# Cross-attention and quantised feed-forward on one core: x normalised in rows and passed through a scratch in device memory

## What is computed

```python
def _layernorm(x, axis=-1, eps=1e-05):
    ...
x = x + _L0_xattn_ref(_layernorm(x), ctx, ctx, w, b, mask)
#   scores = einsum('bqd,bkd->bqk', q1, key) / 0.72
#   attn = softmax(scores) * drop_mask
#   (einsum('bqk,bkd->bqd', attn, value) + bias) @ weights
x = x + _L0_ffn_ref(_layernorm(x), weight_q, weight_scale, ffn_bias)
#   x rounded row by row to 8-bit integers, times weight_q.T, scaled back
```

## Time and profile before

| | us |
|---|---|
| three runs, median (lowest to highest) | 340.8 (340.61 to 341.39) |
| the profiled execution | 341.07 |
| its span from first to last instruction | 339.3 |
| PE busy | 329.1 (97%) |
| DVE busy | 308.6 (91%) |
| ACT busy | 226.8 (67%) |
| POOL busy | 236.4 (70%) |
| DMA queue of SP, share of 16 engines | 51.9% |

### The profile page before, as it was taken

The page is one execution under the profiler, slowest core; times in us unless marked ns, Lnnn a source line. Parts: engine busy times, 40 slices in busy tenths (PEclk is TensorE's granted clock), DMA queues, the critical chain, the costliest instruction groups (busy, mean ns, idle before and its releaser), DMA issues.

```text
span 339.3 us, 6055 instructions
## 1 busy us (share of the span) xinstructions
PE 329.1 (97%) x1574; PEld 263.3 (78%) x1574; DVE 308.6 (91%) x630; ACT 226.8 (67%) x455; POOL 236.4 (70%) x368
## 2 busy tenths in 40 slices
PE   6999999999999999999999999999999999999992
PEld 6988777778777788877778887777888877787781
DVE  3697899999899999999999999999999999999887
ACT  4456676766667786666777767667776666777651
POOL 4175567778777777877777787877777877767642
PEclk9999999999999999999999999999999999999999
DMA  7939854445665544556654555565454556400002
GB/s 237 285 100 251 183 139 117 121 127 163 128 172 153 139 148 123 160 133 170 169 139 131 135 153 140 153 170 150 130 136 140 151 143 170 139 33 31 31 33 94
DMA packets 64545, 47.67 MB, mean 140 GB/s; under 512 B 20112, under 2 KB 51088, under 8 KB 64528
## 3 DMA queue, kind: packets, MB, share of 16 engines
q1 hardware_dynamic: 64528, 47.47, 51.9%
HBM read 35.13 MB, written 8.39 MB: 128 GB/s over the span
## 4 chain that ended last, share of the span: by engine, by line
PE 70%; DVE 9%; issue 1%; ACT 1%; DMA 1%; DVEq 0%; SPq 0%
PE ps_attn L515 7%; PE ps_scores L515 7%; PE ps_scores L517 7%; PE ps_scores L516 7%; PE ps_attn L517 7%; PE ps_attn L516 7%; PE ps_ffn L676 7%; PE ps_vw L515 6%; PE ps_vw L516 6%; PE ps_vw L517 6%; PE ps_pt L507 3%; DVE ffn_out L950 1%; DVE abs_max L963 1%; DMA xq_t<-x_int 1%; PE ps_xt L599 1%
## 5 line engine op out<-in xcount | busy, mean ns | idle before, releaser
L752 ACT ACTIVATE x_norm<-x_blocks,norm_spread 128x128 f32<-128x128 f32 x124 | 51.2, 483 | 2.3 <-ACT norm_spread L745 1.5
L1206 POOL TENSOR_TENSOR ct_lo<-ct_raw,ct_hi 128x512 fp32r<-128x512 f32 x28 | 36.3, 1298 | 23.0 <-ACT ct_hi L730 23.0
L515 PE MATMUL ps_attn<-vw_hi,pt_hi 128*128 128x512 f32 x124 | 51.4, 415 | 0.0
L515 PE MATMUL ps_vw<-w_hi,ct_hi 128*128 128x512 f32 x116 | 50.7, 437 | 0.0
L1159 POOL TENSOR_TENSOR scaled<-meanvar,scale 128x2 f32<-128x2 f32 x32 | 16.6, 517 | 46.6 <-DVE meanvar L913 46.6
L515 PE MATMUL ps_scores<-ct_hi,xt_hi 128*128 128x512 f32 x124 | 48.7, 393 | 0.0
L517 PE MATMUL ps_scores<-ct_hi,xt_lo 128*128 128x512 f32 x124 | 48.5, 391 | 0.0
L516 PE MATMUL ps_scores<-ct_lo,xt_hi 128*128 128x512 f32 x124 | 48.4, 391 | 0.0
L517 PE MATMUL ps_attn<-vw_hi,pt_lo 128*128 128x512 f32 x124 | 48.4, 390 | 0.0
L516 PE MATMUL ps_attn<-vw_lo,pt_hi 128*128 128x512 f32 x124 | 48.3, 389 | 0.0
L854 ACT ACTIVATE x_neg<-x,meanvar 128x512 f32<-128x512 f32 x31 | 22.5, 724 | 38.6 <-DVE meanvar L1122 38.6
(11 more groups left out here) (164 smaller groups left out, 779.5 us busy)
## 6 DMA issues: line engine op xcount, KB each, us to landing
x_in<-in_x_dram SPq DMA_DIRECT2D x32, 256.0 KB, 3.1
mask_in<-in_mask_BxSxS_fk_dram SPq DMA_DIRECT2D x32, 256.0 KB, 3.7
out_dram<-out_tile SPq DMA_DIRECT2D x31, 256.0 KB, 2.2
x_blocks<-in_x_dram SPq DMA_DIRECT2D x60, 128.0 KB, 3.6
ctx_in<-in_ctx_dram SPq DMA_DIRECT2D x56, 128.0 KB, 2.8
ctx_in<-in_ctx_dram SPq DMA_DIRECT2D x4, 256.0 KB, 4.6
x_blocks<-in_L_xattn_weights_dram SPq DMA_DIRECT2D x4, 256.0 KB, 6.5
xq_t<-x_int SPq DMA_TRANSPOSE x26, 2.4
```

Source lines behind the costliest of these rows:

```text
L515: nc.tensor.matmul(bank_, lhs_hi(t), rhs_hi(t), start=(t == 0), stop=False)
L752: last = nc.scalar.activation(x_norm[:, k, a * P:(a + 1) * P], x_blocks[:, slot(n, 4), a * P:(a + 1) * P], ACT.Identity, bias=norm1_spread ...
L1206: nc.gpsimd.tensor_tensor(ct_lo[:, batch_of(n), :, j * P:(j + 1) * P], ct_raw[:, slot(n, 2), :, :], ct_hi[:, batch_of(n), :, j * P:(j + 1) ...
```

## The change

x is no longer loaded a second time. ACT normalises `x_in` in rows, in one instruction of 512 columns with the row's own mean and scale, three tiles ahead of the step, behind `pt_hi` where it stood ahead of it. SP stores the 64K numbers of the tile into `norm_rows`, a scratch in device memory (`store_rows`), behind the mask of the same step; at the beginning of its next step, behind the DMA of the integers, it waits for that store and loads the tile back with its blocks exchanged (`load_rows`, four DMAs of 64 KB for each tile where there were four of 128 KB for two). DVE turns `x_blocks` directly. The matmul L599, ACT's copy L745, POOL's `norm1_masked` (L1175) and the two constants behind them are gone. POOL gets two waits for `x_norm_ready`, of tiles n - 4 and d. (The `skipped` argument goes because only the context still uses `wait_pair`; its numbers stay.)

```diff
-def wait_pair(eng, sems, base, n, skipped=0):
-    uses = (PHASE + n) // 4 + 1 - skipped
+def wait_pair(eng, sems, base, n):
+    uses = (PHASE + n) // 4
     eng.wait_ge(sems[slot(n, 4) // 2], base * (4 * QUADS) + (16 * uses - 4 * PHASE) * QUADS)
+def wait_blocks(eng, sems, base, n):
+    eng.wait_ge(sems[slot(n, 2)], base * (8 * QUADS) + 8 * QUADS * (n + n % 2))
+def wait_rows(eng, sem, base, n):
+    if isinstance(base, int):
+        if base + n > 0:
+            eng.wait_ge(sem, 16 * (base + n))
+    else:
+        assert LOOP_FIRST + n > 0
+        eng.wait_ge(sem, base * 16 + 16 * n)
...
+    norm_rows = nc.dram_tensor("norm_rows", [TILES * P, D], F32, kind="Internal").ap()
...
+            def store_rows(base, n, row):
+                wait_count(sp, x_norm_ready, base, n + 1)
+                sp.dma_start(norm_rows[bass.ds(row, P), :], x_norm[:, slot(n, 2), :]).then_inc(norm_rows_stored, 16)
+            def load_rows(base, n, row):
+                quads = norm_rows[bass.ds(row, P), :].rearrange("(a i) d -> i a d", i=BLOCK)
+                wait_rows(sp, norm_rows_stored, base, n)
+                for b in range(QUADS):
+                    blocks = x_blocks[b * BLOCK:(b + 1) * BLOCK, slot(n, 4), :]
+                    sp.dma_start(blocks.rearrange("i (a c) -> i a c", a=QUADS),
+                                 quads[:, :, b * P:(b + 1) * P]).then_inc(x_blocks_loaded[slot(n, 2)], 16)
...
+            store_rows(0, 1, 1 * P)
             sp.wait_ge(w_lo_ready, NT)
             sp.wait_ge(bias_terms_ready, NT)
-            load_blocks(x_blocks, x_rows, 1 * P, 1, 1, x_blocks_loaded)
-            load_blocks(x_blocks, x_rows, 2 * P, 2, 2, x_blocks_loaded)
+            load_rows(0, 1, 1 * P)
...
+                n = d + 1
+                if exists(base, n) and not is_tile(base, n, 1):
+                    load_rows(base, n, row + n * P)
...
-                n = d + 3
-                if n % 2 == 0 and exists(base, n):
-                    wait_count(sp, x_norm_ready, base, n - 4 + 2)
-                    load_blocks(x_blocks, x_rows, row + n * P, n, 2, x_blocks_loaded)
...
+                n = d + 2
+                if exists(base, n):
+                    store_rows(base, n, row + n * P)
...
-                def spread_norm(n):
-                    wait_count(pe, norm1_masked_ready, base, n)
-                    wait_count(pe, norm1_spread_ready, base, n - 1)
-                    nc.tensor.matmul(ps_xt[:, 0:2 * QUADS], same_lane[:, :],
-                                     norm1_masked[:, slot(n, 2), :, :].rearrange("p a c -> p (a c)"),
-                                     start=True, stop=True).then_inc(spread_done, 1)
-                if is_tile(base, d, 0):
-                    pe.wait_ge(xt_lo_ready, 1)
-                    pe.wait_ge(same_lane_ready, 2 * QUADS - 1)
-                    spread_norm(d + 1)
-                elif exists(base, d + 2):
-                    spread_norm(d + 2)
...
-            def normalise_first():
-                act.wait_ge(norm1_ready, 1)
-                nc.scalar.activation(x_norm[:, 0, :], x_in[:, 0, :], ACT.Identity, bias=norm1[:, 0, 1:2],
-                                     scale=norm1[:, 0, 0:1]).then_inc(x_norm_ready, 1)
             def normalise(base, n):
-                k = slot(n, 2)
-                wait_count(act, spread_done, base, n)
-                wait_count(act, x_norm_ready, base, n - 1)
-                nc.scalar.activation(norm1_spread[:, k, :, :].rearrange("p a c -> p (a c)"), ps_xt[:, 0:2 * QUADS],
-                                     ACT.Copy).then_inc(norm1_spread_ready, 1)
-                wait_count(act, norm1_spread_ready, base, n)
-                wait_pair(act, x_blocks_loaded, base, n)
-                wait_count(act, xt_raw_ready, base, n - 2)
-                for a in range(QUADS):
-                    last = nc.scalar.activation(x_norm[:, k, a * P:(a + 1) * P],
-                                                x_blocks[:, slot(n, 4), a * P:(a + 1) * P], ACT.Identity,
-                                                bias=norm1_spread[:, k, a, 1:2],
-                                                scale=norm1_spread[:, k, a, 0:1])
-                last.then_inc(x_norm_ready, 1)
+                k = slot(n, 4)
+                wait_count(act, norm1_ready, base, n + 1)
+                wait_rows(act, norm_rows_stored, base, n - 2)
+                nc.scalar.activation(x_norm[:, slot(n, 2), :], x_in[:, slot(n, 8), :], ACT.Identity,
+                                     bias=norm1[:, k, 1:2], scale=norm1[:, k, 0:1]).then_inc(x_norm_ready, 1)
...
+            normalise(HEAD, PER_BATCH + 1)
...
-                    normalise(base, d + 1)
+                    normalise(base, d + 2)
...
-                if exists(base, d + 2):
-                    normalise(base, d + 2)
...
+                if exists(base, d + 3):
+                    normalise(base, d + 3)
...
-                wait_count(dve, x_norm_ready, base, n + 1)
+                wait_blocks(dve, x_blocks_loaded, base, n)
                 wait_count(dve, xt_lo_ready, base, n - 1)
-                turn_blocks(xt_raw[:, slot(n, 2), :, :], x_norm[:, slot(n, 2), :], xt_raw_ready)
+                turn_blocks(xt_raw[:, slot(n, 2), :, :], x_blocks[:, slot(n, 4), :], xt_raw_ready)
...
+                wait_count(pool, x_norm_ready, base, n - 4 + 1)
...
-                wait_count(pool, spread_done, base, n - 2)
-                nc.gpsimd.tensor_tensor(norm1_masked[:, slot(n, 2), :, :],
-                                        norm1[:, k, :].rearrange("p (a c) -> p a c", a=1).to_broadcast([P, QUADS, 2]),
-                                        own_block[:, :, :], ALU.mult).then_inc(norm1_masked_ready, 1)
...
-                        pool.wait_ge(x_norm_ready, 1)
+                    wait_count(pool, x_norm_ready, base, d + 1)
...
```

31 lines of the change are left out of this document (4 added, 27 removed).

## The result

| | before | after |
|---|---|---|
| median of its runs | 340.83 (340.61 to 341.39, 4 runs) | 345.61 (343.48 to 347.46, 4 runs) |
| the profiled execution | 341.07 | 343.48 |
| span | 339.3 | 341.7 |

The ratio of the times is 1.014, with a 95% interval of 1.008 to 1.020: the changed kernel is slower, by 4.8 us at the median. The prediction had the sign, with 342.1 and a range to 345.5; the median lies 0.1 us beyond the range and 3.5 above the forecast. The profiled execution, against which the sum was made, is the fastest of the four: 1.4 us above the sum's 342.07. It accounts for the first part of the miss; the second, 2.1 us between it and the median, has no trace of its own. Two single runs in the experiments, 348.4 us of e7_head_store_first and 345.2 of the kernel before beside e4_store_first, fell in the chip's slower state, and the ratios leave them out.

What follows compares the result with a forecast made beforehand. PE was taken to bound the kernel, with DVE 0.1 us a step behind it and DVE the chain in the head. Sum: 341.07 + 3.85 (head) - 2.35 (loop) - 0.5 (tail) = 342.07, so 342.1 us; range 339.0 to 345.5.

Steps and rivals of the forecast that it cites:

- the loop's gain of 2.35 us: Step 6 to step 28: from 216.56 us to 214.2 at DVE's pace, about 0.8 of it in step 6.
- Two bounds 0.1 us apart: Loop: PE's steps take 9.78 us, DVE's own pace is 9.71, so the change relieves only one bound.
- SP in the loop: Even steps: context's fourth DMA issued at 4.75 us, landed at 7.55, needed at 8.17; cover 0.6, cost nothing.
- Rival B: Loop: context late in every even step, from a landing of 3.4 us on; 344.3 to 352 us, chance 0.16.
- SP in the head: Head: tile 2's store lands after 5.0 us, delaying the loads behind it; head ends 3.85 us later.
- a sign of being wrong: Prediction wrong if step 28 comes before 299 us and the head's stretch is under 2.8 us late.
- ring order: Head: tile 2's store can't land ahead of the second constant, at 29.3 us; delay at least 3.35 us.
- ACT, covered by 0.25: Loop: ACT's normalising instruction ends by 197.1 us, ahead of the centring at 197.34; no cost.
- The rows of x, covered by a step: Loop: rows loaded back a step ahead of their use, covered by over 3 us.
- The tail: Tail: two small matmuls leave PE's chain; gain 0.5 us, range 0 to 0.6.
- Rival C: Loop: integers' DMA lands late behind the store of rows; 344.3 us, or about 352; chance 0.09.
- Rival A: Head: tile 2's store lands early, deciding at 4.0 us after issue; 339.3 or 337.3 us, chance 0.24.

Runs made afterwards that it cites:

- e7_head_store_first: Changed kernel, loop order unchanged, with the head's context loads of tiles 6 and 7 right behind the store of tile 1: 341.34 us, ratio 1.001.
- e4_store_first: Changed kernel with context ahead of rows in the loop's even steps, and early context loads behind tile 1's store in the head: 337.62 us, ratio 0.989.
- b1_no_spread: Kernel before without its small matmul L599, that part of the normalisation left out: 339.34 us, ratio 0.994.
- e2_loop: Changed kernel with the context's four loads issued ahead of the rows in the loop's even steps, head unchanged: 341.58 us, ratio 1.002.
- b2_two_spreads: Kernel before with its small matmul L599 done twice: 346.97 us, ratio 1.016.
- again: The changed kernel as it stands, measured once more with a second trace: 344.96 us, ratio 1.011 to the kernel before.
- e1_head: Changed kernel with the context of tiles 6 and 7 loaded early in the head, ahead of the first store of rows: 343.34 us, ratio 1.005.
- e5_split_weights: As e4_store_first, with two of the four transposes of wq_t issued in step 0 while tile 2's store is in flight: 338.28 us, ratio 0.993.

## Why the prediction was right in its sign and off in its size

The step that failed is the cover of 0.6 us that the prediction gave the context's loads in the loop. It was 0 to 0.3, and the loop's gain of 2.35 us came to 0.86. That is 1.5 us; the further 2.1 between the trace and the median stay open (below).

**Two bounds 0.1 us apart: right.** b1_no_spread and e2_loop put DVE's pace at 9.64 to 9.77 us in ordinary steps, 9.69 and 9.70 in the mean (9.71 was worked out), b2_two_spreads shows PE's. The loop without other trouble takes 214.02 against 214.2.

**SP in the loop, "cover 0.6 us, cost nothing": this is the step that failed.** The deadline was right, and the landing nearly: 2.75 to 3.2 us for the last of the four in the loop of the kernel after, 2.9 at the median, for 2.8. The time of its issue was not: 4.75 us behind the integers' DMA in the sum, 5.1 to 5.2 in the ordinary even steps of the kernel after, 5.5 to 5.9 in steps 6, 8, 12 and 20. It landed at 7.8 to 8.3 and at 8.5 to 9.0, against a deadline of 8.17. So the true cover was 0.3 us at best and none in the others. Three things went in:

- A group of four loads is not the time to the next group. The rows take 1.99, as estimated with 1.85, but the context's first DMA stands 2.19 behind the first of the rows (80.16 - 77.97). The pause of 0.2 between groups was left out.
- One even step was taken for all. The trace of before had the other kind: in the first even step of a later pass its context starts 2.0 us behind the integers' instead of 1.4, with its last issue at 136.2 and the integers' at 132.68, so 3.5 behind, where the ordinary step has 3.0. The prediction looked at a single step. The first row below is that of before's step at 132.68, the second that of its step at 172.18:

```profile
L392 SPq DMA_DIRECT2D ctx_in<-in_ctx_dram x4: 316/324/333, 134.7 to 136.2; - x4
...
L392 SPq DMA_DIRECT2D ctx_in<-in_ctx_dram x4: 316/324/423, 173.6 to 175.2; - x4
```

- In the burst ahead of step 6 one issue takes 1.1 to 1.8 us in all nine traces of changed orders. Before it had no more than 0.48 among the context's DMAs of the loop. It fell on the context where that stood second in the burst (1.10 in the kernel after, 1.58 in again, 1.08 in e1_head, 1.79 in e7_head_store_first) and on the rows where these stood second (1.46 in e2_loop, 1.62 in e4_store_first, 1.35 to 1.44 in the three others). There a step of cover hides it. The long issue itself could not be predicted from the trace of before; that a cover of 0.6 us is thin could.

Rival B gave the loop's loss the right resource and half of the mechanism. It decided by the landing ("from 3.4 on"). In the kernel after the last landings stayed at 2.75 to 3.2 and the issue was late; but in again one took 3.7 us behind an issue in time (a wait of 0.69), and in e7_head_store_first one took 4.1 (0.86), which is what B said. Its other unknown, the issue, should have had a range of its own.

**SP in the head: the right sum by two errors, and by luck.** The 3.72 for 3.85 is that of one execution: the same head came to step 6 only 2.3 us late in again and 2.4 in e2_loop, under the 2.8 that the prediction had named as a sign of being wrong. The order of the chain was as written: store, rows, weights' transposes, rows, context. The terms were not. SP in the head of the kernel after:

```profile
24.22 0.34 SPq L403 DMA_DIRECT2D norm_rows<-x_norm  x1
28.28 1.75 SPq L411 DMA_DIRECT2D x_blocks<-norm_rows  x4
...
31.50 5.35 SPq L478 DMA_TRANSPOSE wq_t<-wq_rows  x4
36.90 2.00 SPq L411 DMA_DIRECT2D x_blocks<-norm_rows  x4
```

The store was issued 0.6 earlier than assumed and landed in 4.0 instead of 5.0; the transposes took 5.35 instead of 6.58. The context's last DMA took 4.0 to land, not 3.1, at the end of eight issues in a row since 36.9 (3.1 in again). The landings, from the DMA issues of 24.2, of 40.4 and of 42.5:

```profile
norm_rows<-x_norm SPq DMA_DIRECT2D x1, 256.0 KB, 4.0
...
ctx_in<-in_ctx_dram SPq DMA_DIRECT2D x1, 128.0 KB, 4.0
...
xq_t<-x_int SPq DMA_TRANSPOSE x1, 4.2
```
So DVE began the context at 44.46, 2.40 later than before, and not 3.85. The rest came from a place that the prediction had put down as covered: the first integers' DMA, issued at 42.49 into the same burst, took 4.2 us, and PE stood still for it. PE in order of time, and then PE, PEld, DVE, ACT and POOL busy, granted clock (0.72), DMA share and GB/s from 46 to 52 us:

```profile
46.82 1.02 PE L680 MATMUL ps_ffn<-wq_t,xq_t 128*128 128x512 bf16 x4 [3.36 <-DMA xq_t<-x_int]
...
50.49 0.63 PE L538 MATMUL ps_vw<-w_hi,ct_lo 128*128 128x512 f32 x1
50.92 0.63 PE L536 MATMUL ps_vw<-w_hi,ct_hi 128*128 128x512 f32 x1
...
52.06 0.39 PE L536 MATMUL ps_vw<-w_hi,ct_hi 128*128 128x512 f32 x1
52.29 0.39 PE L537 MATMUL ps_vw<-w_lo,ct_hi 128*128 128x512 f32 x1
```

```profile
46.00:52.00 6.00, 4.30 (x14) 3.11 (x15) 5.63 (x12) 3.21 (x7) 4.19 (x7) 0.72 0.45 132
```

After that pause, matmuls start every 0.43 us up to 51.8, on the lower of TensorE's two levels (1.2 GHz), and every 0.23 after it. Steps 2 to 3 took 10.47 instead of 9.95. With 0.70 of the late context in step 6 this makes up nearly all of the head's 3.72. In again, where PE's pause was 1.90 us, the clock of that stretch stayed at 1.00 and the step at 9.94; in e2_loop, with 3.24, it was 0.72 and 10.60. So a late DMA can cost PE more than its lateness. What length of pause it takes these traces don't say: behind the pause of 1.31 us at 25 us, with 0 to 1.4 us of idling just ahead of it, the clock fell in five of the eight traces of changed orders that have it and stayed in three. e7_head_store_first and e4_store_first have no pause for the integers of over 0.8 us here, and the full clock.

From the Trainium skill's "DMA: Bandwidth & Descriptors" ("Queues, rings and completion order") the prediction took that descriptors of one queue are consumed in ring order on each DMA engine, and concluded that the store can't land ahead of the constant, hence a delay of at least 3.35 by 29.3. (Ring order alone doesn't say that; the section adds that a transfer's completion is marked only behind the earlier writes of the same DMA engine, and that transfers on different numbers of DMA engines may complete out of order.) The delay was 2.40, below that bound, and yet the trace agrees with the rule: the constant was issued at 22.90 and landed in 4.7 us, at 27.6, and the store landed behind it, at 28.2. What was wrong was the price put into it, the 5.8 us of another burst; the errors behind it, of the transposes and of the context's landing, nearly cancel. The rule's turn of mind, that a store waits for what is ahead of it in the queue, is what e1_head (512 KB ahead: 6.8 us) and e4_store_first (512 KB behind: 4.0) show.

**ACT, covered by 0.25: right, with little to spare.** `x_norm` takes 0.82 us and ends 0.15 us ahead of the centring. **POOL: right**, nothing. **The rows of x, covered by a step: right** in the loop. **The tail: right**, -0.45 for -0.5.

**Rival C** (the integers land late) shows in the page's 4.3 us of PE waiting, of which 3.36 are the head's one; in the loop of the kernel after they are 0.16 to 0.23 us each in five steps, and DVE's pace covers them. In e4_store_first PE waited longer twice, 0.70 and 1.10 us, and the steps behind them took 10.20 and 10.45: that is the 1.0 us by which its loop is longer than that of e5_split_weights. **Rival A** was the right question (what the store's landing is), and its turning point of 4.0 was just met; but with the landing at 4.0 the head still lost 2.4 to DVE's context: its last load landed 1.5 us earlier than in the sum, where A's 339.3 needed 2.8.

**What stays open.** The changed kernel's median lies 1.8 to 2.1 us above its profiled execution, in both sets of runs. Two things can vary. The waits for the context do between its traces (2.3 us in five steps of one, 3.1 in five of the other), and so does the clock, which was lower in the slower executions of again; in the first four executions of the changed kernel the two don't go together (346.8 us at 0.990, 344.5 at 0.985). The runs without a trace don't show which of the two it is. Also, b1_no_spread gains 1.8 us on the kernel before and e4_store_first 3.5, with loops that differ by 0.4; their intervals touch. The profiled execution of e4_store_first, 339.3, is 1.7 above its median, about 1.1 of it by the clock in the first step. Part may also be the start: the second tile of x was waited for 0.8 us in the profiled execution of before and 1.4 to 3.3 in those of the experiments. What makes a single issue on SP take 1.1 to 1.8 us was not found, nor why the clock falls behind the pause at 25 us in one execution and not in the other.

## What to carry to other kernels

An engine's queue of DMA issues has deadlines like any engine: work out the time of the last issue ahead of each deadline in every kind of step (the first one of a pass too), with the pauses between groups, and take less than half a microsecond of cover as none. Order the issues of a step by deadline, and put a store that something waits for in front of the loads, which then pass the time in which the queue waits for its landing. Where two engines are within 1% of each other, removing work from one gives the difference only, here 0.1 of 0.24 us; the rest of the gain has to be defended on the other resources that the change loads.

## What the runs showed of the hardware that was not expected

- SP's issue of a DMA in the loop takes 0.32 to 0.48 us with few exceptions, whether it moves 64, 128 or 256 KB; so splitting a load in two doubles what it costs in the queue. In the burst of nine ahead of step 6 one took 1.1 to 1.8 us, in all nine traces of changed orders and in none of the three with the order of before. In four of the nine a mask's issue near 108 us took 1.2 to 1.5.
- A store of 256 KB landed in 2.1 to 4.0 us with 512 KB issued behind it (four traces), and in 6.6 to 6.8 with the same 512 KB ahead of it (two). Over all steps its median is 3.0 to 3.4, where the stores of results have 2.2.
- TensorE's clock fell to the lower level after a pause of PE of 3.24 and of 3.36 us in the head and not after one of 1.90 at the same place; but elsewhere in the head, behind a pause of 1.31 us, it fell in five traces of the changed orders and not in three, and the first step took 1.0 to 1.1 us longer where it fell.
